# Scan rows: diagonal part added first, one gate multiply on VectorE, GpSimd's gate products removed

## The reference

```
y = ssd(xs, dt, A, Bm, Cm)          # Y_diag + Y_off, per chunk of 128 tokens
y = y + D_param[None, None, :, None] * xs
y = y.reshape(B, L, D_INNER)        # D_INNER = 512
y = rmsnorm(y * jax.nn.silu(z), mixer_norm_w)
h1 = res + y @ out_proj_w
```

## Time and profile before

| | |
|---|---|
| median of 3 runs | 735.2 us (733.47 to 735.37) |
| the profiled execution | 736.37 us, its span 734.6 us |
| PE busy | 690.5 us (94%) |
| DVE busy | 589.9 us (80%) |
| ACT busy | 237.6 us (32%) |
| POOL busy | 245.5 us (33%) |
| mean granted clock of TensorE | 0.977 of full speed |

### The profile page before, as it was taken

One profiled execution on the slowest core, in us unless ns is written; L12 is line 12 of the kernel. 1 busy time (PEld: TensorE's weight loads), 2 busy tenths in 40 slices (PEclk: granted clock), 3 DMA queues, 4 the chain that ended last, 5 costly groups with the idle time before them and its releaser, 6 DMA issues.

```text
span 734.6 us, 10099 instructions
## 1 busy us (share of the span) xinstructions
PE 690.5 (94%) x2797; PEld 441.0 (60%) x2798; DVE 589.9 (80%) x1473; ACT 237.6 (32%) x479; POOL 245.5 (33%) x395
## 2 busy tenths in 40 slices
PE   5978879999999989999969999999999999999995
PEld 4445665568556766675864666666665555555564
DVE  4899988977867585376775888999998898888882
ACT  1576747586376445223102111111111111111110
POOL 2133442533323233320011233333333343434333
PEclk8999979999999999999989999999999999999999
DMA  9232000300030036014117881111143343435112
GB/s 317 62 111 116 0 1 1 116 0 1 31 143 1 1 117 240 1 56 153 33 40 279 283 254 27 30 29 29 29 129 80 102 114 87 130 63 153 30 23 29
DMA packets 39350, 63.20 MB, mean 86 GB/s; under 512 B 5456, under 2 KB 29072, under 8 KB 39312
## 3 DMA queue, kind: packets, MB, share of 16 engines
q1 hardware_dynamic: 31824, 52.61, 20.6%
q0 software_dynamic: 7488, 10.11, 8.5%
HBM read 52.88 MB, written 9.83 MB: 85 GB/s over the span
## 4 chain that ended last, share of the span: by engine, by line
PE 69%; DVE 17%; issue 5%; POOL 3%; ACT 3%; DMA 3%; POOLq 0%; DVEq 0%; ACTq 0%
PE ps L1089 23%; PE ps L1110 12%; PE ps L759 4%; PE ps L771 4%; PE ps L453 3%; PE ps L1098 3%; PE ps L508 3%; PE ps L575 3%; PE ps L785 3%; DVE big L1642 2%; DVE big L1662 2%; DMA out_rows<-big 2%; PE ps L522 2%; PE ps L632 2%; DVE big L2241 2%
## 5 line engine op out<-in xcount | busy, mean ns | idle before, releaser
L2241 DVE STREAM_TRANSPOSE big<-big 32x224 f32<-32x224 f32 x560 | 225.5, 403 | 8.4
L1089 PE MATMUL ps<-big 128*128 x512 | 200.1, 544 | 1.4 <-ACT big L1544 0.7
L1089 PEld LDWEIGHTS ps<-big 128*128 128x128 f32 x512 | 97.0, 191 | 89.5 <-issue 87.9
L1110 PE MATMUL ps<-big 128*128 x448 | 102.2, 380 | 1.0 <-DVE big L2241 0.6
L1550 ACT ACTIVATE big<-ps 128x896 f32<-128x896 f32 x36 | 33.0, 917 | 202.5 <-PE ps L1089 179.3
L1110 PEld LDWEIGHTS ps<-big 128*128 128x128 f32 x448 | 82.7, 190 | 11.7 <-issue 1.8
L2292 POOL TENSOR_TENSOR big<-big 128x1 f32<-128x1 f32 x110 | 22.0, 200 | 164.4 <-DVE big L2231 147.2
L453 PEld LDWEIGHTS ps<-big 128*128 128x128 f32 x319 | 39.6, 144 | 38.9 <-issue 26.5
L453 PE MATMUL ps<-big 128*128 128x128 f32 x319 | 52.1, 277 | 8.6 <-ACT big L1192 2.3
L1642 DVE SCALAR_TENSOR_TENSOR big<-ps,big 128x511 f32<-128x511 f32 (+2 forms) x72 | 53.0, 747 | 6.6 <-ACT big L1211 4.8
L2490 POOL DMA_INDIRECT out_rows<-big x32 | 51.4, 1605 | 20.8 <-issue 20.8
(11 more groups left out here) (232 smaller groups left out, 1011.9 us busy)
## 6 DMA issues: line engine op xcount, KB each, us to landing
big<-in_w SPq DMA_DIRECT2D x36, 896.0 KB, 7.8
big<-cum_rows SPq DMA_DIRECT2D x16, 512.0 KB, 5.5
out_rows<-big SPq DMA_DIRECT2D x4, 512.0 KB, 3.0
xn_rows<-big SPq DMA_DIRECT2D x4, 512.0 KB, 3.1
big<-in_hidden SPq DMA_DIRECT2D x1, 1536.0 KB, 12.4
big<-in_in_proj SPq DMA_DIRECT2D x1, 1288.0 KB, 7.4
big<-in_gate SPq DMA_DIRECT2D x1, 640.0 KB, 13.2
big<-in_up SPq DMA_DIRECT2D x1, 640.0 KB, 8.6
```

The lines of the kernel that those rows point to most:

```text
L1089: last = mm(bank(bk + n)[:, 0:HALF], xT[:, k, :], expert_cols(e, off + k * M + n * HALF, HALF), start=(k == 0), stop=(k == KD - 1))
L1110: last = mm(bank(7)[:, 0:D], hTs[:, half, j * P:(j + 1) * P], expert_cols(e, 2 * KD * M + j * D, D), start=(j == 0), stop=(j == MB - 1))
L2241: last = V.transpose(hTs[c * SQ:(c + 1) * SQ, half, :].rearrange("p (j t) -> p j t", j=MB)[:, :, q * SQ:(q + 1) * SQ], ha[q * SQ:(q + 1) * ...
```

## The change

VectorE's `y_` first adds the bank DIAG to the sum of the other two parts in yb (in chunk 0: to xsd, into yb) and then multiplies yb once by the gate. The first step now waits for y2_ready (chunk 0: xsd_ready), the second for the gate. GpSimd's `gated` and its 16 calls are gone, and with them the tile's use (its columns stay reserved) and the semaphore y3_ready.

```diff
             def y_(n, c):
                 v.wait_ge(y_ps, nth(n, CH, c))
+                if c == 0:
+                    v.wait_ge(xsd_ready, nth(n, CH, c))
+                    if n > 0:
+                        v.wait_ge(yT_taken, nth(n - 1, CH, 2))
+                        v.wait_ge(ssy_ready, nth(n - 1, CH, 2))
+                    V.tensor_tensor(yb[:, 0, :], bank(DIAG), xsd[:, 0, :], ALU.add).then_inc(y_taken, 1)
+                else:
+                    v.wait_ge(y2_ready, nth(n, CH - 1, c - 1))
+                    V.tensor_tensor(yb[:, c % 2, :], yb[:, c % 2, :], bank(DIAG), ALU.add).then_inc(y_taken, 1)
+                v.wait_ge(y_taken, nth(n, CH, c))
                 v.wait_ge(z_taken, nth(n, CH, c))
-                if n + c > 0:
-                    v.wait_ge(y4_ready, n * CH + c)
-                V.tensor_tensor(yz, bank(DIAG), sz[n % 2][:, c, :], ALU.mult).then_inc(y_taken, 1)
-                v.wait_ge(y_taken, nth(n, CH, c))
-                v.wait_ge(y3_ready, nth(n, CH, c))
-                V.tensor_tensor(yb[:, c % 2, :], yb[:, c % 2, :], yz, ALU.add).then_inc(y4_ready, 1)
+                V.tensor_tensor(yb[:, c % 2, :], yb[:, c % 2, :], sz[n % 2][:, c, :], ALU.mult).then_inc(y4_ready, 1)
...
-            def gated(n, c):
-                g.wait_ge(z_taken, nth(n, CH, c))
-                if c == 0:
-                    g.wait_ge(xsd_ready, nth(n, CH, c))
-                    if n > 0:
-                        g.wait_ge(yT_taken, nth(n - 1, CH, 2))
-                        g.wait_ge(ssy_ready, nth(n - 1, CH, 2))
-                    G.tensor_tensor(yb[:, 0, :], xsd[:, 0, :], sz[n % 2][:, 0, :], ALU.mult).then_inc(y3_ready, 1)
-                else:
-                    g.wait_ge(y2_ready, nth(n, CH - 1, c - 1))
-                    G.tensor_tensor(yb[:, c % 2, :], yb[:, c % 2, :], sz[n % 2][:, c, :], ALU.mult).then_inc(y3_ready, 1)
...
             scaled_x(0, 1)
 
-            gated(0, 0)
             decayed_x(0, 1)
```

More of the change, by code:

```diff
@@ L167, in build @@
         gm = cols(CH, P)
-        yz = cols(INNER)
+        cols(INNER)
         em = (em_even, cols(CH, HEADS * P))
@@ L311, in build @@
         xdt_ready, xdtd_ready, xsd_ready, em_ready = map(sem, ("xdt_ready", "xdtd_ready", "xsd_ready", "em_ready"))
-        off_ps, off_scaled, y_ps, y_taken, s_ps, s_taken, y2_ready, y3_ready, y4_ready, ssy_ready, ry_ready = map(sem, ("off_ps", "off_scaled", "y_ps", "y_taken", "s_ps", "s_taken", "y2_ready", "y3_ready", "y4_ready", "ssy_ready", "ry_ready"))
+        off_ps, off_scaled, y_ps, y_taken, s_ps, s_taken, y2_ready, y4_ready, ssy_ready, ry_ready = map(sem, ("off_ps", "off_scaled", "y_ps", "y_taken", "s_ps", "s_taken", "y2_ready", "y4_ready", "ssy_ready", "ry_ready"))
         yT_ps, yT_taken, o_ps, o_taken, xh_ready, ssh_ready, rh_ready = map(sem, ("yT_ps", "yT_taken", "o_ps", "o_taken", "xh_ready", "ssh_ready", "rh_ready"))
@@ L2378, in _ @@
             plus_x_D(0, 1)
-            gated(0, 1)
             scale_y(0, 0)
@@ L2383, in _ @@
             scaled_x(0, 3)
-            gated(0, 2)
             scale_y(0, 1)
             plus_x_D(0, 3)
-            gated(0, 3)
             scale_y(0, 2)
@@ L2392, in _ @@
             decayed_x(1, 0)
-            gated(1, 0)
             scale_y(0, 3)
@@ L2401, in _ @@
             plus_x_D(1, 1)
-            gated(1, 1)
             decayed_x(1, 2)
@@ L2406, in _ @@
             plus_x_D(1, 2)
-            gated(1, 2)
             scaled_x(1, 3)
@@ L2411, in _ @@
             plus_x_D(1, 3)
-            gated(1, 3)
             scale_y(1, 2)
@@ L2416, in _ @@
             decayed_x(2, 0)
-            gated(2, 0)
             scale_y(1, 3)
@@ L2426, in _ @@
             plus_x_D(2, 1)
-            gated(2, 1)
             scale_y(2, 0)
             plus_x_D(2, 2)
-            gated(2, 2)
             scale_y(2, 1)
@@ L2436, in _ @@
             plus_x_D(2, 3)
-            gated(2, 3)
             decayed_x(3, 0)
             scale_y(2, 2)
-            gated(3, 0)
             scale_y(2, 3)
@@ L2448, in _ @@
             plus_x_D(3, 1)
-            gated(3, 1)
             scale_y(3, 0)
@@ L2455, in _ @@
             plus_x_D(3, 2)
-            gated(3, 2)
             plus_x_D(3, 3)
             scale_y(3, 1)
-            gated(3, 3)
             scale_y(3, 2)
```

## The result

The changed kernel is faster by 1.0%.

What follows compares the result with a forecast made beforehand. TensorE, busy 94% of the span, bounds the kernel, with VectorE's queue setting the pace from 80 to 100 us. Gains of 3.3 + 0.4 + 0.7 + 0.9 + 0.4 = 5.7 us from 735.2 give 729.5 us, range 725.5 to 732.8.

Steps and rivals of the forecast that it cites:

- (a): Sequence 0: L1622 and L1624, stretched under gate product L2339 and its follower L2325, give back 0.63 us.
- (b): Sequence 0: L1684 takes 1.01 us instead of 0.69; 0.32 us comes back.
- (d): Sequence 0: four L1662 from 93.40 us take 1.88 us instead of 0.86; 1.02 us comes back.
- (e): Sequence 0: L1714 at 97.48 us, 1.19 us instead of 0.43 under L2318, will miss it; 0.76 us comes back.
- Term (c): Sequence 0: eight L1662 from 83.08 us, with 1.76 us of blockage, give back 0.6 us, ends 0 and 1.04.
- A sign that failed: Sequence 0: if the forecast is right, no L1662 of more than 1.1 us around 84 and 93 us.
- Rival 2: GpSimd's blocks move to VectorE's next SBUF instruction instead of vanishing: gain 3.0 us, time 732.2 us, chance 0.16.
- Sequence 0 in all: Five collisions ahead of L482 at 99.4 us sum to 3.3 us, between 2.2 and 4.0.
- 158, 201, 255 us and h1_: TensorE's waits at 158 us, at 201 us, before L785 and before L575 shrink by 0.4, 0.7, 0.9, 0.4 us.
- rival 1: The slow clock of about 10 us behind the wait before L482 shortens too: 2.5 us, time 727.0, chance 0.30.
- rival 4: TensorE's clock falls at a new place, a spell of 10 us costing 5: near 734.5 us, chance 0.08.
- Rival 3: VectorE's first step waits for plus_x_D: up to 8.2 us lost against 5.7, time 737.7, from nine chunks, chance 0.04.

Runs made afterwards that it cites:

- e5: A second profile of the same changed kernel, taken with the experiments: 729.2 us, span 727.4 us.
- after's first profile: The first profiled execution of the changed kernel, the slowest of its four runs: 730.28 us, span 728.5 us.
- the filled pair: The kernel before and the changed kernel, each with unused matmuls ahead of L482 in sequences 1 and 2: 733.47 us (0.9975) and 729.19 us (0.9909).

## Why the prediction was right, and which terms were off

Point by point, forecast against the table above:

- **Terms (a), (b), (d), (e)**: 0.63, 0.32, 1.02 and 0.76 forecast; 0.61, 0.32, 1.01 and 0.77 measured. These are places where the trace of before showed one instruction blocked and its undisturbed time beside it. For (e) the prediction had the right cause as well, two instructions that miss each other.
- **Term (c)**: mis-sized, 0.6 forecast, 1.09 measured, a little over its upper end of 1.04. The prediction read the eight L1662 rightly, 1.76 us of blockage before, and foresaw that VectorE would gain 0.33 us on GpSimd here and that two GpSimd instructions would still fall on them. They did, and the eight gave back nothing (3.48 us both times). What it left out was L1673 ahead of them, which is stretched before by 1.08 us under plus_x_D: by those 0.33 us it now begins first. That the term came out so near its upper end, by a block that was not in it, is luck.
- **A sign that failed**: no L1662 of more than 1.1 us was to be left around 84 and 93 us. At 93 that came true, but at 81.28 us e5 has one of 1.3 us, under plus_x_D. The forecast did not hang on it, since term (c) had allowed for nothing to be gained there.
- **Rival 2** (the blocks move): so it went at the eight L1662 and, as the forecast had counted, at L1622 (1.02 us instead of 1.25), and nowhere else in sequence 0.
- **Sequence 0 in all**: 3.3 forecast, 3.8 measured (3.57 and the 0.23 by which e5 was late at 40 us). L482 was expected near 96 us and starts at 95.86 (96.86 in after's first profile). The prediction gives the sum as between 2.2 and 4.0 and later moves it by 1.1 either way, which would be 4.4 at the top.
- **158, 201, 255 us and h1_**: 0.4, 0.7, 0.9, 0.4 forecast; 0.50, 0.63, 1.04, 0.23 measured. The last was forecast from the wait before L575 of diag (3,1), which fell only from 0.84 to 0.72 us.
- **The clock**: forecast at no gain in the likeliest case, and priced at 2.5 in rival 1 with a chance of 0.30. At 100 us it brought about 2.4 in e5, at the place that the rival named, and gave 1.4 back at 263 us, where a new stretch begins (rival 4, at a third of its price of 5). That the stretch shortens with the wait is borne out by every profile here: it is 10.2 us where the wait before L482 is 2.8 (before, and the change in sequences 1 to 3 alone), and 3.4 or 6.8 us where it is 1.0 to 1.1. Why it is the one or the other is open. So the outcome was the sum and part of rival 1. The prediction had the sign at hand: in the trace of before the slow stretch begins 0.1 us behind the end of the longest wait that the change shortens.
- **Rival 3**: the first step waits in 2 places, not the nine from which it would decide; old order and new order time alike.

The sum of 5.7 for the gaps stands beside 6.2 read from the table (3.8 + 0.5 + 0.63 + 1.04 + 0.23) and 4.9 (2.7 either way) from the filled pair. With the clock's 2.4 less 1.4 the table gives 7.2, the difference of the spans. The median came 1.4 us under the forecast. That is less than the interval of its ratio, 2.3 us either way, so timing does not tell it from nothing; the profiles would put 0.5 of it to term (c) and 1.0 to the clock.

**After's first profile** lies 1.1 us of span above e5's. Its early slow stretch comes 3 us sooner and lasts 10.2 us, over the small matmuls of L482 and the L508 behind them:

```profile
45.92 1.12 PE L453 MATMUL ps<-big 128*128 128x128 f32 x4 [1.84 <-ACT big L1192]
46.83 3.42 PE L482 MATMUL ps<-big 128*128 128x8 f32 x16
```

Before had 0.66 and 1.85 us for the two, after the same wait (1.83). L508 starts 2.03 us later there than in before, and part of this is taken up by the wait at L494. The change touches nothing ahead of it. Why the clock falls at 45 us in one execution and at 48 in another with the same gap ahead is open; the profiles show both positions for kernels that are alike up to there, so it is not the change. This profile gains less at 100 us, since its stretch there is 6.8 us, and loses nothing at 263 us.

## What to carry to other kernels

A GpSimd instruction with long rows can cost twice: its own time, and that of a VectorE instruction with all operands in SBUF that starts under it. Here VectorE's tensor_tensor, tensor_scalar and scalar_tensor_tensor instructions were stretched so, by up to 1.09 us. Where VectorE sets the pace, find the stretched instructions (the longest of a line against its median), look which GpSimd instruction lies over each, and count the difference, because it is on the path even if nobody waits for GpSimd. Then look which of the two engines comes first at each pair that stays: a shift of 0.33 us turned a stretched VectorE instruction into a stretched GpSimd one. VectorE steps with one operand in PSUM kept their time under any of them, and GpSimd steps of one to four columns did not stretch it visibly. If a change shortens the wait ahead of a stretch at TensorE's lower clock, count part of that stretch as gained, and look at the next long gap for part of it lost.

## What the runs showed of the hardware that was not expected

- Narrow GpSimd instructions do not block visibly. VectorE's four L1662 took 0.86 us under two GpSimd powers of 128x1 (0.57 and 0.62 us long) and 1.90 under one multiply of 128x512 (1.27 us). Under a multiply of 128x4 one L1662 took 0.29 us, and 1.13 under a multiply of 128x512.
- Who starts first decides who is held up. L1673 took 2.30 us where plus_x_D had begun 0.14 us before it, and 1.22 where L1673 began 0.19 us before plus_x_D, which then took 2.16 us instead of 1.35.
- Not every VectorE instruction on SBUF is stretched. In the trace of before, BATCH_NORM_STATS2 at 42.99 us took 0.41 us under the scaling of 42.96, as elsewhere (0.41), and RECIPROCAL at 58.77 took 0.35 under L2325.
- A PSUM reader on VectorE is indifferent to GpSimd also where it runs under a wide instruction from its start: L1697 at 247.26 took 0.69 us under L2330.
- Filling one TensorE gap with idle matmuls can cost more than it saves. In the one profile of it, a stretch of 3.4 us at the lower clock at 48 us was gone, the next wait grew from 1.59 to 2.87 us, and the clock fell there for 10.2 us. By the ratios the kernel lost 3.2 us, 2.8 either way.
